# Modulation rows computed once in a prologue and loaded per batch with a broadcast, in a two-layer attention and mixture-of-experts kernel

## The reference

```python
mod = (_silu(c) @ wmod).reshape(16, 6, 1, -1)
sa, ca, ga, sb, cb, gb = (mod[:, i] for i in range(6))
ga = (2 * (ga >= 0) - 1) * jnp.maximum(jnp.abs(ga), 0.25)      # gb alike
h = _layernorm(x) * (1 + ca) + sa
x = x + ga * attention(h)
h = _layernorm(x) * (1 + cb) + sb
x = x + gb * ffn(h)
```

## Time and profile before

| | us |
|---|---|
| median of 3 runs | 2350.81 |
| lowest and highest run | 2305.39, 2354.41 |
| profiled execution, first to last instruction | 2378.5 |

### The profile page before, as it was taken

One profiled execution on the slowest core, in us unless ns is written; L12 is line 12 of the kernel. 1 busy time (PEld: TensorE's weight loads), 2 busy tenths in 40 slices (PEclk: granted clock), 3 DMA queues, 4 the chain that ended last, 5 costly groups with the idle time before them and its releaser, 6 DMA issues.

```text
span 2378.5 us, 35332 instructions
## 1 busy us (share of the span) xinstructions
PE 2162.3 (91%) x11152; PEld 1350.9 (57%) x11152; DVE 1141.0 (48%) x4250; ACT 894.1 (38%) x1820; POOL 404.1 (17%) x643
## 2 busy tenths in 40 slices
PE   5999999879999999999989999969999999999490
PEld 3666666545555555555557888844555555554260
DVE  3344545354444444443428888845554545444102
ACT  1243434423343344343452222214554444554130
POOL 2111211121111121121100000022121212121505
PEclk8598989957686788786889999958998999999595
DMA  6000000000000000000000000010000000000132
GB/s 211 1 1 1 0 1 0 1 0 1 1 1 2 1 1 2 1 1 1 1 1 1 1 0 0 1 36 1 1 1 2 1 2 1 1 1 2 48 107 75
DMA packets 26218, 30.38 MB, mean 13 GB/s; under 512 B 3744, under 2 KB 19392, under 8 KB 25664
## 3 DMA queue, kind: packets, MB, share of 16 engines
q1 hardware_dynamic: 24000, 24.08, 3.2%
q0 software_dynamic: 2048, 4.20, 0.6%
HBM read 19.88 MB, written 8.39 MB: 12 GB/s over the span
## 4 chain that ended last, share of the span: by engine, by line
PE 86%; DVE 4%; issue 3%; POOL 2%; ACT 2%; another core or an unknown queue 1%; DMA 1%; SPq 0%; POOLq 0%; DVEq 0%; ACTq 0%
PE ps_out L1812 25%; PE ps_four L1794 8%; PE ps_four L997 5%; PE ps_max L1008 5%; PE ps_max L1764 4%; PE ps_max L1759 3%; PE ps_four L1718 3%; PE ps_four L1674 3%; PE ps_work L1699 3%; PE ps_max L1760 2%; PE ps_four L1699 2%; PE ps_work L1679 2%; PE ps_four L1787 2%; PE ps_four L1796 2%; PE ps_work L1658 2%
## 5 line engine op out<-in xcount | busy, mean ns | idle before, releaser
L1812 PE MATMUL ps_out<-attn_f,v_all 128*9 128x256 f32 (+3 forms) x2560 | 654.7, 384 | 5.8 <-ACT attn_f L1383 5.2
L1394 ACT ACTIVATE attn_f<-ps_four 128x384 f32<-128x384 f32 (+1 forms) x640 | 340.5, 532 | 627.2 <-PE ps_four L1796 618.4
L1812 PEld LDWEIGHTS ps_out<-attn_f,v_all 128*9 128x9 f32 (+1 forms) x2560 | 196.1, 96 | 273.9 <-issue 78.1
L1794 PE MATMUL ps_four<-q_st,k_st 26*128 26x256 f32 (+1 forms) x640 | 263.3, 411 | 0.2 <-DVE q_st L1602 0.2
L1581 DVE CUSTOM_DVE_ANT_0 ps_max<-ps_max,q_masks 128x128 f32<-128x128 f32 (+1 forms) x768 | 256.2, 377 | 0.0
L1588 DVE TENSOR_REDUCE row_max<-ps_max 128x2 f32<-128x512 f32 x256 | 170.1, 686 | 132.7 <-PE ps_max L1764 132.6
L1383 ACT COPY attn_f<-ps_out 9x512 f32<-9x512 f32 (+1 forms) x320 | 183.8, 575 | 132.1 <-PE ps_out L1812 132.1
L1794 PEld LDWEIGHTS ps_four<-q_st,k_st 26*128 26x128 f32 (+1 forms) x640 | 127.8, 200 | 75.6 <-issue 26.2
L1796 PE MATMUL ps_four<-q_st,k_st 26*128 26x256 f32 (+2 forms) x640 | 164.8, 258 | 0.0
L1574 DVE COPY wait_cell<-one 128x1 f32<-128x1 f32 x384 | 56.9, 148 | 186.3 <-PE ps_max L1760 181.2
L1008 PEld LDWEIGHTS ps_max<-wd,o_both 128*128 128x128 f32 x1024 | 134.7, 193 | 18.7 <-DVE o_both L904 8.3
(11 more groups left out here) (250 smaller groups left out, 3423.0 us busy)
## 6 DMA issues: line engine op xcount, KB each, us to landing
wd<-in_L_ffn_W SPq DMA_DIRECT2D x16, 256.0 KB, 2.6
gates_all<-in_select SPq DMA_DIRECT2D x3, 1024.0 KB, 7.3
x_all<-in_L_attn_x SPq DMA_DIRECT2D x8, 256.0 KB, 6.0
slots_dram<-attn_f SPq DMA_DIRECT2D x8, 256.0 KB, 5.5
h_tok<-slots_dram SPq DMA_DIRECT2D x8, 256.0 KB, 2.7
y_dram<-o_both SPq DMA_DIRECT2D x8, 256.0 KB, 2.4
out_x<-x_all SPq DMA_DIRECT2D x16, 128.0 KB
wgu<-in_L_ffn_Wg SPq DMA_DIRECT2D x1, 1024.0 KB, 5.8
```

The lines of the kernel that those rows point to most:

```text
L1394: nc.scalar.activation(probs[:, h % 4, 0:w], ps_exp[:, h % 3, 0:w], ACT.Exp, scale=c.scale).then_inc(exp_done, 1)
L1794: nc.tensor.matmul(bank[:, 0:S], k_st[rows, r, g, 0:P], q_st[rows, r, g, :], start=not c.causal, stop=True, skip_group_check=True)
L1812: last = nc.tensor.matmul(ps_out[0:c.hd + 1, (h % 2) * S + first:(h % 2 + 1) * S], v_tok[c.index][:, r, kb, kv, :], probs[:, h % 4, kb * S ...
```

## The change

The modulation rows of both layers and all batches are computed once. In the prologue two more matmuls on PE multiply `silu_c` (16 columns) with the last 512 columns of `wmod`, one for each layer, into 16 partitions; ACT copies them into `mod_rows`, and DVE makes the gates out of them on 16 partitions (`mod_gates`, eight instructions, at the end of c0's start). SP stores `mod_rows` to `mod_dram`. Then SP loads, for each batch of each pass, its rows into the ring `mod` with a broadcast over 128 partitions, and for each layer the expert gates of all 16 batches into `gates_all` in one broadcast of 1 MB.

The step "mod" goes on every engine, and with it `c_bcast` and `gate_tmp`. Readers of `mod` and `gates_all` on DVE wait for the loads (`mod_load[r]`, `gates_load`). The additions of eps on POOL read a copy that DVE makes (128x2). `order(c)` has a name less and the three fixed places are `(1, 4, 5)`, so steps move in the table and change their bank.

```diff
-        PREP = ["stat", "mod", "xhat", "sq", "hn", "ht", "q", "k", "qd", "v", "sel0", "sel1", "sel2", "sel3"]
+        PREP = ["stat", "xhat", "sq", "hn", "ht", "q", "k", "qd", "v", "sel0", "sel1", "sel2", "sel3"]
...
-            return (["stat", "mod", "combine", "xhat", "ot"] + (["sq", "y", "hn", "ht"] if c.index == 1 else ["ht", "y"])
+            return (["stat", "combine", "xhat", "ot"] + (["sq", "y", "hn", "ht"] if c.index == 1 else ["ht", "y"])
...
-                    at = (1, 3, 4)[j]
+                    at = (1, 4, 5)[j]
...
+            act.wait_ge(pro_pe, 4)
+            nc.scalar.copy(mod_rows.rearrange("b l k d -> b l (k d)"), ps_four[0:NB, 0:2, :]
+                           ).then_inc(mod_rows_out, 1)
...
+            for layer in range(2):
+                last = nc.tensor.matmul(ps_four[0:NB, layer, :], silu_c[:, layer, :], wmod[:, layer, 2 * D:],
+                                        start=True, stop=True)
             last.then_inc(pro_pe, 1)
...
+            def load_select(n):
                 sp.wait_ge(select_ready, n)
-                if n == 2:
-                    sp.wait_ge(moe_done, NB // 2)
                 sp.dma_start(stage_sel, sel_dram[:, n]).then_inc(sel_load, 16)
+
+            def load_gates(layer):
+                sp.wait_ge(select_ready, layer + 2)
+                sp.dma_start(gates_all[:], mod_dram[layer, :, 3, :].partition_broadcast(P)).then_inc(gates_load, 16)
+
+            def load_mod(c, b, r):
+
+                n = n_of(c, b)
+                if c.index == 1 and not isinstance(b, int):
+                    sp.wait_ge(h_done, b - RING + 1)
+                elif c.index == 2 and not isinstance(b, int):
+                    sp.wait_ge(rt_h, b - RING + 1)
+                elif c.index < 2 and not (c.index == 0 and isinstance(b, int)):
+                    sp.wait_ge(y_out, n - RING + 1)
+                lo, hi = c.parts
+                sp.dma_start(mod[:, r, 0:hi - lo, :],
+                             mod_dram[c.layer, bass.ds(b, 1), lo:hi, :].rearrange("o k d -> (o k) d").partition_broadcast(P)
+                             ).then_inc(mod_load[r], 16)
...
+            sp.wait_ge(mod_rows_dve, 3)
+            sp.dma_start(mod_dram.rearrange("l b k d -> b l k d"), mod_rows).then_inc(mod_store, 16)
+            sp.wait_ge(mod_store, 16)
+            for r in range(RING):
+                load_mod(CFGS[0], r, r)
+            load_select(1)
+            load_later_mods(CFGS[0])
+            for r in range(RING):
+                load_mod(CFGS[1], r, r)
+            load_gates(0)
+            load_later_mods(CFGS[1])
+            sp.wait_ge(moe_done, NB // 2)
+            load_select(2)
+            for r in range(RING):
+                load_mod(CFGS[2], r, r)
+            load_gates(1)
+            load_later_mods(CFGS[2])
             sp_tail(sp)
...
-                if name == "mod":
-                    dve.wait_ge(mod_out, n + 1)
-                    for g, part in enumerate(c.gates):
...
+                        dve.wait_ge(mod_load[r], 4 * (n - r) + 16)
                         nc.vector.tensor_tensor(y_tok[:, r2], y, mod[:, r, 0:1, :].to_broadcast([P, BLK, D]),
                                                 ALU.mult).then_inc(y_out, 1)
...
-                if name == "mod":
-
-                    pe.wait_ge(c_bcast_done, n + 1)
-                    nc.tensor.matmul(bank[:, 0:c.parts * D], c_bcast[:, r2, :],
-                                     wmod[:, c.layer, c.mod:c.mod + c.parts * D],
-                                     start=True, stop=True).then_inc(mod_mm, 1)
```

More of the change, by code:

```diff
@@ L35, with __init__ @@
 class Attn:
-    def __init__(self, index, layer, mod, heads, kv, causal, window, scale):
+    def __init__(self, index, layer, heads, kv, causal, window, scale):
         self.index = index
         self.layer = layer
-        self.mod = mod
-        self.parts = (1, 3, 4)[index]
-        self.gates = ((0,), (2,), (0, 3))[index]
+        self.parts = ((0, 1), (1, 3), (0, 3))[index]
         self.heads = heads
@@ L298, in adaln_two_layers @@
         res_done = sem("res_done")
-        c_bcast_done = sem("c_bcast_done")
-        mod_mm = sem("mod_mm")
-        mod_out = sem("mod_out")
-        mod_scale = sem("mod_scale")
-        gate_a = sem("gate_a")
-        gate_b = sem("gate_b")
-        gate_done = sem("gate_done")
+        mod_rows_out = sem("mod_rows_out")
+        mod_rows_dve = sem("mod_rows_dve")
+        mod_store = sem("mod_store")
+        mod_load = [sem("mod_load%d" % r) for r in range(RING)]
+        gates_load = sem("gates_load")
         stats_done = sem("stats_done")
@@ L1158, in prep @@
                                             ALU.pow).then_inc(rstd_done, 1)
-                if name == "mod" and c.index > 0:
-                    pool.wait_ge(mod_out, n + 1)
-                    scale = mod[:, r, c.index, :]
-                    nc.gpsimd.tensor_tensor(scale, scale, one[:].to_broadcast([P, D]), ALU.add).then_inc(mod_scale, 1)
                 if c.index == 1:
@@ L1273, in prep @@
                 n, r2 = n_of(c, b), r % 2
-                if name == "mod":
-                    act.wait_ge(mod_mm, n + 1)
-                    at_least(act, y_out, n - RING + 1)
-                    if c.index == 2:
-                        at_least(act, rt_h, b - RING + 1)
-                    nc.scalar.copy(mod[:, r, 0:c.parts, :].rearrange("p a d -> p (a d)"),
-                                   work[bank_of(c, name)][:, 0:c.parts * D]).then_inc(mod_out, 1)
                 if name == "sq":
@@ L1603, in maxima, with mod_gates @@
                                             ALU.add).then_inc(place_done, 1)
+            def mod_gates():
+                gates = [mod_rows[:, layer, 0::3, :] for layer in range(2)]
+                dve.wait_ge(mod_rows_out, 1)
+                nc.vector.tensor_scalar(mod_rows[:, :, 2, :], mod_rows[:, :, 2, :], 1.0, None, ALU.add)
+                for layer in range(2):
+                    nc.vector.tensor_scalar(gate_rows[:, 0, layer], gates[layer], 0.0, 0.5, ALU.is_ge, ALU.subtract)
+                    last = nc.vector.scalar_tensor_tensor(gate_rows[:, 1, layer], gates[layer], -1.0, gates[layer],
+                                                          ALU.mult, ALU.max)
+                last.then_inc(mod_rows_dve, 1)
+                dve.wait_ge(mod_rows_dve, 1)
+                nc.vector.tensor_scalar(gate_rows[:, 1], gate_rows[:, 1], 0.25, 2.0, ALU.max, ALU.mult
+                                        ).then_inc(mod_rows_dve, 1)
+                dve.wait_ge(mod_rows_dve, 2)
+                for layer in range(2):
+                    last = nc.vector.tensor_tensor(gates[layer], gate_rows[:, 0, layer], gate_rows[:, 1, layer], ALU.mult)
+                last.then_inc(mod_rows_dve, 1)
             def start(c):
@@ L1617, in start @@
                     maxima(c, 0, 0, name)
+                if c.index == 0:
+                    mod_gates()
             def segment(c, b, r):
@@ L1869, in start @@
                 else:
-                    free = {0: (y_out, c.first), 1: (o_done, c.first)}
+                    free = {0: (y_out, c.first), 1: (y_out, c.first)}
                 post_step, prep_step, maxima_step = tracked(free)
```

50 lines of the change are left out of this document (20 added, 30 removed).

## The result

| | before | after |
|---|---|---|
| median | 2337.0 us (4 runs) | 2509.4 us (4 runs) |
| lowest to highest | 2305.4 to 2354.4 | 2466.9 to 2520.3 |
| profiled execution, span | 2378.5 us | 2518.5 us |

The ratio is 1.072, with a 95% interval of 1.051 to 1.094 (the medians alone give 1.074): the change makes the kernel slower by 7%. The profiled execution itself took 2520.3 us, 1.8 more than its span.

A forecast was written before the change was run, and what follows sets the result against it. PE's work and its clock were taken to bound the kernel. Work and waits gave -22 us and the clock +108, taking 2378.5 to 2464.5 us, 2436 on the median; range 2290 to 2530.

The forecast's parts named there:

- a clock that falls in every batch of c0: Rival, far end of the forecast: slower by clock drops in all c0 batches, 2525 us, 2495 on the median; no separate chance.
- What mod gave back: PE in all passes: removed matmuls save 38 us, starts of c1 and c2 save 8, prologue adds 1.
- The wait of ot in c0: c0, ot directly behind combine: PE waits 0.9 us for DVE, costing 0.84 us in each of 15 batches, 12.6 us.
- c0's clock: c0: eight batches get a stretch of 17.07 us at the lower clock, costing 68 us; bounds 0 to 128.
- The wait of q in c1: c1, q soon after ht: PE waits on ACT's copy, 0.5 us in each of 15 batches, 7.5 us; bounds 0 and 15.
- c1's clock: c1: 60 us more at the lower clock as dense mod ahead of combine goes, costing 30 us; bounds -30 and +100.
- c2: c2: 20 us more at the lower clock, costing 10 us, bounds -20 and +50; moved steps there cost 3 us more.
- Half speed: All passes: a microsecond at the lower clock does half the work, so 606 us there cost about 303.
- The clock as it was: Rival: the clock stays unchanged and only work and waits count, 2356.5 us, 2329 on the median, -0.9%; chance 0.18.
- The clock gets better: Rival: a third of c1's and c2's lower-clock time goes, 84 us more gained, 2273 us, 2246 on the median; chance 0.21.
- Late loads: Rival: y of first batches waits for broadcast loads on DVE, some 7.3 us per place; chance 0.04.
- That the removed matmuls were hidden: Rival: mod's removal on PE gains nothing, only new waits remain, 2402 us, 2375 on the median, +1%; chance 0.04.

The follow-up runs named there:

- three pairs of kernels: Kernels with mod kept against those with it removed and loaded, in old slots, new slots and mixed table; spans less 0.43 of lower-clock time differ by 43, 44, 44 us.
- the two batches above: A c1 batch of the changed kernel wholly at 0.50, 62.79 us; one with q put back, 37.29 us with 3.03 at 0.50.
- another table: Hand-written slots, mixed from the shortest passes so far: changed kernel 2270.8 us, ratio 0.959 to before; kernel before with mod kept 2316.3 us, 0.980 by medians.

## Why the prediction was right, and where it wasn't

The forecast was slower, 2436 us in a range of 2290 to 2530, through the clock. It was slower through the clock, 2509. The direction and the mechanism are shown. The size is in part luck: the forecast was +3.6% and the result +7.2%, near the upper end, and of the two large terms one was too large and the other far too small. The rival that came nearest, a clock that falls in every batch of c0 (2495), has the wrong pass. In the two profiles, with the clock taken out, the three stretches are 30 us shorter than before, where the sum had -22; at the lower clock they have 434 us more, times 0.43 187 us, where it had +108; and the opening's clock, which it didn't have, gives 15 back. By its own steps:

*What mod gave back.* 38 us on PE and 8 at the starts, less 1. With the clock taken out it is 43 to 44 us in three pairs of kernels. Its parts were not as forecast: the matmuls alone are 28, not 38. The rest was measured only as a whole; besides the starts, PE had waited 10.0 us in 13 places for `c_bcast` before (waits of the weight loads counted), a term that the prediction doesn't have. The time with all old slots doesn't show it, since the clock takes back 38 us there. The loads are of up to 192 KB, not 128; nothing waited for them.

*The wait of ot in c0.* Forecast 0.84 us a batch more, from an idle time of 0.90. The idle time after is 0.90, to the digit, and ot starts 1.97 us behind combine, where 1.98 was forecast. That the nearest row was the end of the pass, where nothing stands between, made this exact.

*c0's clock.* Forecast eight drops of 17.07 us. There were ten, one in nearly every steady batch, but of 6.83 us mostly: the clock came back much sooner than at the loop's edge. y and q stand ahead of the rise; that they bring it was not tried here. The term was mis-sized, 68 us forecast and 38 measured: 89 us more at 0.50, times 0.43. Without the clock c0 is 3.5 us longer, where 12.6 - 6.3 = 6.3 was forecast for the waits less the 15 x 0.42 of mod's work. Filling the wait and moving ot away both raise c0's clock to 0.97, so the mechanism is shown.

*The wait of q in c1.* Forecast 7.5 us, 0.5 a batch. It was 3.3 us in 13 places. The step that failed is that I priced this move by its wait. Its real price is the clock: with q alone put back c1 is 128 us shorter. What I had for c1's clock, 30 us (bounds -30 and +100), was argued from the missing mod ahead of combine, "Of that stretch mod [...] is the dense part, and it goes". That reason was wrong: with mod kept and the slots moved c1 is as long (885 us), and with mod gone and the slots kept it is shorter than before (716 in that profile). c1 is 116 us longer; the clock's part is (672 - 370) x 0.43 = 130 us against the 30 forecast, beyond the bound of 100 too. The difference lies at the rises, which come later, and not at the falls, of which it has fewer (11 against 15). I had read where the clock falls, and not what stands ahead of where it rises; q directly behind the values was one of these places, and the diff of the order showed that it went.

*c2.* Forecast 20 us more at the lower clock, 10 us of time. With the experts and the end of the pass before it is 42 us more, 18 us of time, and the stretch is 1.1 us shorter all the same; the removed work and the shorter start are in it.

*Half speed.* I took a microsecond at the lower clock as half of the work. By the two batches above, 62.79 us and some 36 at full clock, it does 0.57 of the work. Why it isn't 0.50 was not looked into; the combine matmuls of 36 columns follow one another at 213 ns against 112, the values at 392 against 216 (medians in c1 of the changed kernel), so the short ones are no exception.

*The rivals.* The clock as it was: c0's 0.84 against 0.94 says no. The clock gets better: no, in the changed kernel; but as a statement on the slots it has something, since another table brings 2% with mod kept and 4% without it. That table brings some 30 us beside the clock as well (2001 against 2032 and 2045 against 2075). Late loads: no wait on them. That the removed matmuls were hidden: not so, by the three pairs.

*The rules of the Trainium skill.* The page "TensorE: Matmul & The Clock Gate" says in its section on psum-queue depth-cycling that short idles between groups of matmuls make the clock go up and down. c0 looks like this: waits of 0.90 us, and the drops ended when the wait was filled. In c1 the clock stayed low with PE busy for 167.25 of 167.25 us, which neither that section nor "Why this matters for your kernels" would give. The prediction took the fall at 617.50, with no idle time ahead of it, as agreeing with the first of the two; it agrees with neither. What PE is given to do counts there, not whether it is busy: q or two dense matmuls behind the values brought the clock back.

## What to carry to other kernels

Where the granted clock is well below 1, list what stands ahead of each fall and of each rise before you move anything: a step that costs nothing by its waits can be the one that brings the clock back. When a change shortens a list from which the slots are worked out, separate the two with a name that does nothing; here the removal alone changed nothing on balance, and the slots cost 7 to 9%. Before you call removed work worthless, take the clock out: two batches at different clocks give its price, and here 43 us of work had been saved and 38 lost to the clock. And a wait of under a microsecond in a dense stretch may be worth filling, even with work that nobody reads.

## What the runs showed of the hardware

PE at 1.2 GHz was busy without a gap for whole batches, and stayed there for up to 167 us on end, so a busy engine doesn't by itself bring the clock back. An idle time of 0.90 us behind eight short matmuls went with a drop, mostly of 6.83 us, in ten batches of c0; in the first two, and at the end of c0 before, the same wait had none at once. With 1.77 us of matmuls in that place, or with ot moved away, only the drops at the loop's edges were left. Two matmuls of 512 columns directly behind the values stood ahead of eight of fourteen rises in one pass and raised its clock from 0.62 to 0.79. A microsecond at the lower clock cost 0.43 us in these kernels. Runs of one kernel lie up to 6% apart (2418 to 2568 us), and nearly all of it is the time at the lower clock. c1 with its old slots took 716, 748 and 789 us in three kernels, 765 and 766 in the two that keep mod whole; a difference under 2% in one profile says little here.
